# Decoder layer on one Trainium2 core: attention loop laid out anew, twelve units of maxima ahead, times-V product in front of the scores

## The reference, cut to what matters

```
x = layernorm(x + attn_block(x))          # gives x1
x = layernorm(x + xattn(x, ctx))          # gives x2
x = layernorm(x + experts(x))
# xattn, 16 heads of 8 features:
q = rope(layernorm_per_head(x @ q_w.T + q_b)) * scale
k = layernorm_per_head(ctx @ k_w.T + k_b);  v = ctx @ v_w.T + v_b
o = softmax(q @ k.T) @ v
return o @ out_w.T + out_b
```

## Time and profile before

| what | value |
|---|---|
| median of 3 runs | 373.38 us (371.13 to 375.3) |
| the profiled execution's own time | 370.08 us |
| its span, first to last instruction | 368.0 us |
| mean granted TensorE clock | 0.853 |
| PE busy, share of span | 276.7 us, 75% |
| DVE busy | 186.6 us, 51% |
| ACT busy | 154.7 us, 42% |
| POOL busy | 95.6 us, 26% |

### The profile page before, as it was taken

How to read it: one execution, slowest core, us unless ns; L and a number is a source line. 1 busy time by engine, 2 the same in 40 slices (tenths; PEclk the granted TensorE clock), 3 DMA queues, 4 the chain that set the end, 5 groups by cost and what they waited for, 6 DMA issues and landing times.

```text
span 368.0 us, 7297 instructions
## 1 busy us (share of the span) xinstructions
PE 276.7 (75%) x2437; PEld 210.3 (57%) x2437; DVE 186.6 (51%) x660; ACT 154.7 (42%) x365; POOL 95.6 (26%) x126
## 2 busy tenths in 40 slices
PE   1798967589799268899876988741058999999880
PEld 0588755447558135344443545431055999999880
DVE  4541556611153475654797596557100656566560
ACT  2233244455783425654672465410107443434330
POOL 2000036204232222220341403105100343535341
PEclk9999998599899666955995699865559999999996
DMA  7700025305993944335055000001864000000000
GB/s 221 234 2 1 0 62 144 52 0 133 233 285 97 215 109 116 49 89 89 2 152 80 32 3 18 16 2 37 198 177 112 7 14 21 16 15 15 5 14 14
DMA packets 30529, 28.34 MB, mean 77 GB/s; under 512 B 2829, under 2 KB 27024, under 8 KB 30498
## 3 DMA queue, kind: packets, MB, share of 16 engines
q1 hardware_dynamic: 28884, 25.24, 28.9%
q0 software_dynamic: 1328, 2.66, 2.2%
q10 hardware_dynamic: 288, 0.07, 0.1%
HBM read 17.85 MB, written 10.37 MB: 77 GB/s over the span
## 4 chain that ended last, share of the span: by engine, by line
PE 54%; DVE 12%; DMA 11%; ACT 9%; issue 8%; POOL 3%; SPq 1%; POOLq 0%; ACTq 0%; DVEq 0%
PE ps L796 7%; PE ps L787 7%; PE ps L669 4%; DMA out_dram<-ADD,tok_u 4%; PE ps L647 4%; PE ps L385 3%; DVE M L1135 3%; PE ps L556 3%; PE ps L685 2%; PE ps L416 2%; DMA WA<-in_attn_w_dram 2%; PE ps L457 2%; PE ps L393 2%; DMA QPK<-q_packed_scratch 2%; PE ps L707 2%
## 5 line engine op out<-in xcount | busy, mean ns | idle before, releaser
L1135 DVE TENSOR_REDUCE M<-ps 128x4 f32<-128x512 f32 x64 | 43.2, 687 | 30.2 <-PE ps L614 29.9
L962 ACT ACTIVATE CTX<-ps 128x512 f32<-128x512 f32 x64 | 38.1, 599 | 35.8 <-PE ps L647 27.2
L1003 ACT ACTIVATE KPK<-ps,EB 128x128 f32<-128x128 f32 x80 | 24.7, 359 | 41.7 <-PE ps L787 41.7
L796 PE MATMUL ps<-EW,KPK 128*128 128x128 f32 x320 | 40.1, 278 | 0.9 <-ACT KPK L1003 0.8
L1311 DVE TENSOR_SCALAR KPK<-ps,EB 128x128 f32<-128x128 f32 x80 | 22.5, 344 | 34.6 <-PE ps L787 34.4
L787 PE MATMUL ps<-QPK,EW 128*128 x320 | 39.1, 275 | 0.8 <-ACT QPK L988 0.8
L796 PEld LDWEIGHTS ps<-EW,KPK 128*128 128x128 f32 x320 | 38.1, 191 | 1.3 <-ACT KPK L1003 1.0
L787 PEld LDWEIGHTS ps<-QPK,EW 128*128 128x128 f32 x320 | 37.3, 192 | 1.0 <-issue 1.0
L647 PE MATMUL ps<-QPK,KPK 49*128 49x128 bf16 x256 | 28.9, 243 | 8.2 <-DVE M L1135 6.1
L614 PE MATMUL ps<-KPK,QPK 48*128 48x128 bf16 x256 | 27.9, 251 | 8.7 <-DMA QPK<-q_packed_scratch 5.6
L1406 POOL DMA_INDIRECT out_dram<-ADD,tok_u x21 | 21.1, 1004 | 46.3 <-DVE ADD L1304 43.6
(11 more groups left out here) (185 smaller groups left out, 531.5 us busy)
## 6 DMA issues: line engine op xcount, KB each, us to landing
k_packed_scratch<-PART SPq DMA_DIRECT2D x24, 128.0 KB, 2.4
KPK<-k_packed_scratch SPq DMA_DIRECT2D x8, 384.0 KB, 6.4
q_packed_scratch<-PART SPq DMA_DIRECT2D x24, 128.0 KB, 2.4
QPK<-q_packed_scratch SPq DMA_DIRECT2D x8, 384.0 KB, 5.8
KPK<-sorted_scratch SPq DMA_DIRECT2D x13, 198.0 KB, 4.1
EW<-in_eW_dram SPq DMA_DIRECT2D x1, 2048.0 KB, 11.9
sorted_scratch<-XW SPq DMA_DIRECT2D x8, 198.0 KB
X<-in_x_dram SPq DMA_DIRECT2D x4, 256.0 KB, 4.3
```

The lines of the kernel that those rows point to most:

```text
L796: last = mm(ps[:, 4, 0:P], HE[:, c, :], EW2[:, e, c % NF, :], start=(c == 0), stop=(c == 2 * NF - 1))
L962: A(EXPS[:, u % 4, :], ps[:, 2 + u % 2, :], ACT.Exp).then_inc(s_exp, 1)
L1003: last = A(HE[:, c, :], ps[:, k, (c % 2) * P:(c % 2 + 1) * P], ACT.Relu, bias=EB1[:, h, c:c + 1])
L1135: nc.vector.tensor_reduce(M[:, b % RING, c:c + 4], bank_rows(u % 2), AX.X, ALU.max).then_inc(s_max, 1)
```

## The change

Before the loop the maxima of `LEAD` = 12 units are done, and the whole query chains of groups 1, 2 and 3, in an order written out by hand; the two `keep_clock(3)` are gone there. Group 1's rotation goes into the last part of the GELU network's second product, with one more pair of activation table loads around it on ACT. In the loop `times_v(u - 2)` stands in front of `scores(u, u + LEAD)`. `max_T` and `negate_max` are for batch b+2 in unit r = 1 (before: batch b+1 in r = 0). `results_T(b - 2)` is in r = 0 (before: `results_T(b - 1)` in r = 3). `rows_T`, `project`, `ranks` and DVE's steps for the finished groups move one to three units later, and `whole_parts` of group 2 moves behind the loop. The load of the experts' second matrix (EW2) moves behind all the queries' DMAs in SP's list. On POOL the chains of groups 2 and 3 come before `x1_plus_bias(2)`, the load of the experts' bias and its arithmetic. Some PSUM banks change (`head_bank`, `var_bank`, `x1_bank`, `rot_bank`), with the waits that go with them.

```diff
-AHEAD = 2
+LEAD = 12
...
             for g in range(G):
                 write_parts(1, g)
                 read_packed(1, g)
-                if g == 0:
-                    sp.wait_ge(s_f2, G)
-                    sp.dma_start(EW2[:, :, :, :], ...).then_inc(ld_exp, 16)
+            sp.wait_ge(s_f2, G)
+            sp.dma_start(EW2[:, :, :, :], ...).then_inc(ld_exp, 16)
...
                         queries(1)
+                    if j == 2 and g == 3:
+                        rotate(1)
                 last.then_inc(s_f2, 1)
...
             pe.wait_ge(s_g1, NF * G)
-            for b in range(AHEAD):
-                for r in (0, 2):
-                    scores_for_max(4 * b + r)
-                    if (b, r) == (1, 0):
-                        queries(2)
-                if b == 1:
-                    x1_T(3)
-                keep_clock(3)
-                max_T(b)
-                if b == 0:
-                    rotate(1)
-                    x1_T(2)
+            x1_T(2)
+            queries(2)
+            scores_for_max(0)
+            scores_for_max(2)
+            x1_T(3)
+            variances(1, 2)
+            scores_for_max(4)
             queries(3)
+            max_T(0)
+            scores_for_max(6)
+            variances(1, 3)
+            rotate(2)
+            scores_for_max(8)
+            max_T(1)
+            scores_for_max(10)
+            rotate(3)
             for u in range(4 * B):
                 b, r = divmod(u, 4)
-                scores(u, u + 4 * AHEAD)
                 if u >= 2:
                     times_v(u - 2)
-                for g in range(2, G):
-                    if (b, r) == (q_batch(g), 1):
-                        pe.wait_ge(s_negm, b + AHEAD)
-                        variances(1, g)
-                    if (b, r) == (q_batch(g) + 1, 0):
-                        pe.wait_ge(s_lv[1], g + 1)
-                    if (b, r) == (q_batch(g) + 1, 1):
-                        pe.wait_ge(s_negm, b + AHEAD)
-                        rotate(g)
-                    if (b, r) == (q_batch(g) + 2, 0):
-                        pe.wait_ge(s_t2, g + 1)
-                if r == 1 and b > 2 * GB and b % GB == 1:
-                    pe.wait_ge(s_negm, b + AHEAD)
-                    ranks(b // GB - 2)
-                if r == 0 and b > 2 * GB and b % GB == 2:
-                    pe.wait_ge(s_ranked, b // GB - 1)
-                if r == 0 and 1 <= b and b + AHEAD - 1 < B:
-                    max_T(b + AHEAD - 1)
-                if r == 1 and b > GB and b % GB == 1:
-                    rows_T(b // GB - 1)
-                if r == 1 and b > GB and b % GB == 2:
-                    project(b // GB - 1)
-                if r == 3 and b >= 1:
-                    results_T(b - 1)
+                scores(u, u + LEAD)
+                if r == 0 and b >= 2:
+                    results_T(b - 2)
+                if r == 1 and b + 2 < B:
+                    if b > 2 * GB and b % GB == 2:
+                        pe.wait_ge(s_ranked, b // GB - 1)
+                    max_T(b + 2)
+                if r == 2 and b > GB and b % GB == 1:
+                    rows_T(b // GB - 1)
+                if r == 2 and b > GB and b % GB == 2:
+                    project(b // GB - 1)
+                if r == 3 and b > 2 * GB and b % GB == 1:
+                    pe.wait_ge(s_negm, min(b + 3, B))
+                    ranks(b // GB - 2)
             times_v(4 * B - 2)
             times_v(4 * B - 1)
+            results_T(B - 2)
             results_T(B - 1)
...
# ACT, in front of the last GELU of the second product
+                if g == G:
+                    nc.scalar.preload_act_table_set(LN_EXP)
+                    head_inv_std(1, 1)
+                    inv_std(2, 2, 1e-5)
...
# DVE
             first_sum(2)
+            head_norm(1, 1, QBC)
+            normalise_x1(2)
+            add_rotation(1)
             first_sum(3)
-            head_norm(1, 1, QBC)
...
-            for u in range(4 * AHEAD):
+            for u in range(LEAD):
                 maxima(u)
-                if u == 3:
-                    normalise_x1(2)
-                if u == 4:
-                    add_rotation(1)
+                if u == 1:
+                    normalise_x1(3)
                 if u == 5:
-                    normalise_x1(3)
+                    head_norm(1, 2, QBC)
+                if u == 7:
+                    add_rotation(2)
+                    head_norm(1, 3, QBC)
+                if u == 9:
+                    add_rotation(3)
```

More of the change, by code:

```diff
@@ L962, in _ @@
                 A(EXPS[:, u % 4, :], ps[:, 2 + u % 2, :], ACT.Exp).then_inc(s_exp, 1)
+                if u == 0:
+                    middle_part(1, 2)
                 if u == 1:
-                    square(1, 3, s_qc, QBC)
-                for g in range(2, G):
-                    if (b, r) == (q_batch(g), 1):
-                        head_inv_std(1, g)
-                    if (b, r) == (q_batch(g) + 1, 2):
-                        high_part(1, g)
-                    if (b, r) == (q_batch(g) + 2, 0):
-                        middle_part(1, g)
-                if r == 0 and 1 <= b and b + AHEAD - 1 < B:
-                    negate_max(b + AHEAD - 1)
+                    high_part(1, 3)
+                if u == 4:
+                    middle_part(1, 3)
+                if r == 1 and b + 2 < B:
+                    negate_max(b + 2)
                 if r == 2 and b >= 1:
                     copy_results(b - 1)
-                if r == 1 and b > GB and b % GB == 1:
+                if r == 3 and b > GB and b % GB == 1:
                     copy_oT(b // GB - 1)
-                if r == 1 and b > GB and b % GB == 3:
+                if r == 2 and b > GB and b % GB == 3:
                     inv_std_x2(b // GB - 1)
@@ L1221, in _ @@
             for u in range(4 * B):
                 b, r = divmod(u, 4)
-                if u + 4 * AHEAD < 4 * B:
-                    maxima(u + 4 * AHEAD)
-                for g in range(2, G):
-                    if (b, r) == (q_batch(g), 3):
-                        head_norm(1, g, QBC)
-                    if (b, r) == (q_batch(g) + 1, 1):
-                        add_rotation(g)
-                if r == 0 and b >= 2:
+                if u + LEAD < 4 * B:
+                    maxima(u + LEAD)
@@ L1231, in _ @@
+                if r == 1 and b >= 2:
                     attention_rows(b - 2)
[L1232 removed]
+                if r == 3 and b > GB and b % GB == 2:
                     add_x1(b // GB - 1)
[L1234 removed]
+                if r == 0 and b > GB and b % GB == 3:
                     mean_var(lambda b: blk(N, b), 3, b // GB - 1, s_y2)
[L1236 removed]
+                if r == 3 and b > GB and b % GB == 3:
@@ L1237, in _ @@
                     normalise_x2(b // GB - 1)
-                if r == 3 and b > GB and b % GB == 3:
-                    whole_parts(b // GB - 1)
-                if r == 1 and b >= 2 * GB and b % GB == 0:
+                if r == 0 and b >= 2 * GB and b % GB == 0:
+                    whole_parts(b // GB - 2)
+                if r == 2 and b >= 2 * GB and b % GB == 0:
                     experts(b // GB - 2)
-                if r == 3 and b >= 2 * GB and b % GB == 0:
+                if r == 0 and b > 2 * GB and b % GB == 1:
@@ L1243, in _ @@
                     count_experts(b // GB - 2)
-                if r == 2 and b > 2 * GB and b % GB == 1:
+                if r == 0 and b > 2 * GB and b % GB == 2:
                     place(b // GB - 2)
+            whole_parts(G - 2)
             attention_rows(B - 2)
@@ L1367, in _ @@
             query_affine(1)
+            low(1, 1, ADD, KP)
+            query_affine(2)
+            query_affine(3)
+            low(1, 2, ADD, KP)
+            low(1, 3, ADD, KP)
             x1_plus_bias(2)
-            low(1, 1, ADD, KP)
             x1_plus_bias(3)
@@ L1375, in _ @@
             nc.gpsimd.tensor_copy(X2[:, :, P:ROW], token_no[:, :, None].to_broadcast([P, B, ROW - P])).then_inc(s_x2id, 1)
-            for g in range(2, G):
-                query_affine(g)
-                low(1, g, ADD, KP)
             pool.wait_ge(s_qc, G)
```

45 lines of the change are left out of this document (24 added, 21 removed).

## The result

The changed kernel takes 375.38 us (median of 4 executions, 374.15 to 379.25) against 372.25 us of the kernel before (4 executions, 369.58 to 375.3): ratio 1.0216, 95% interval 1.015 to 1.0283. The forecast was 363.7 us, faster; it is slower, though not by much: the medians are 0.8% apart.

What follows compares the result with a forecast made beforehand. PE was taken as the bound at half clock, DVE at full clock. Case 1 summed +2.9 ahead of the loop, batches 28.8 - 35.1, -6.3 and -0.5, +0.5 behind: 373.4 - 9.7 = 363.7 us, range 356 to 378.

Steps and rivals of the forecast that it cites:

- case 1: Loop: clock low at the start, back about batch 3.5, then 1.00; -9.7 us, chance 0.35, the forecast.
- case 4: Loop: clock never back, or lost again; batches 6 to 12 take 48 us, 13 to 15 take 22; +12.3 us, chance 0.12.
- case 3: Loop: clock back only with ranks or projection in batch 9 or 10; +0.3 us, chance 0.18.
- the order put at nothing: Loop units: times-V before scores just covered at 1.00, 1.39 us against PE's 1.38; up to 6 us if semaphores take longer.
- `keep_clock(3)`: Ahead of the loop: removing the two saves PE some 3 us, but PE waits for DVE there anyway.
- DVE as the bound of batches 6 to 12 at 1.00: Batches 6 to 12: 5.35 us each, 37.5 in all, -6.3 us; sign: DVE over 90% busy.
- the stretch ahead of the loop: Before the loop: 17 to 22 us from a start at 126 to 127, so the loop starts 2.9 us later.
- A plain batch at 0.50: Loop: a batch with nothing extra costs PE 5.9 us at half clock; 4.2 at 1.00 with ACT's part.
- The wait for `copy_results`: Loop: `results_T` a batch behind its copy removes PE's 7.2 us of waits.
- the stall in `experts`: Batches 6 to 12: DVE's 1.5 us stall goes, since POOL's bias work comes earlier, at about 155 us.
- The mask row has 7 units to land: Loop: 7 units instead of 3, room for a DMA that now meets EW2's load; no wait for the row.

Runs made afterwards that it cites:

- before_no_keep_clock: The kernel before without its two `keep_clock(3)` ahead of the loop: 369.73 us, ratio 0.982.
- after_fill_loop: The changed kernel with sixteen unread 128x128 matmuls in PE's two waits ahead of the loop and every `results_T` transpose issued twice: 366.83 us, ratio 0.9927.
- scores_first_fill_front: The changed kernel with scores again ahead of times-V and sixteen unread 128x128 matmuls in PE's two waits ahead of the loop: 370.21 us.
- after_fill_front: The changed kernel with 8 unread 128x128 matmuls in each of PE's two waits for DVE ahead of the loop: 370.72 us, ratio 1.0015.
- after_lead8: The changed kernel with maxima 8 instead of 12 units ahead, so a mask row has 3 units to land: 384.16 us, ratio 1.0284.
- before_doubled: The kernel before with every transpose of `results_T` issued twice, nothing else: 363.15 us, ratio 0.9741.
- after_dense_back: The changed kernel with four unread 512-column products, one in each of batches 1 to 4: 370.9 us, ratio 1.0158.
- scores_first_filled: The changed kernel with scores again ahead of times-V, sixteen unread matmuls ahead of the loop and `results_T` transposes doubled: 357.25 us, ratio 0.9559.
- lead8_ew2_early: The changed kernel with maxima 8 instead of 12 units ahead and EW2's load back behind group 0's queries: 377.27 us.

## Why the prediction was wrong

**The step that failed first: the clock's course of case 1, in its second half.** It began as forecast: loop at 0.50, clock back at batch 4.6 (forecast 3.5). Then it said 1.00 for batches 6 to 12, and the clock fell at 193.3, was back at 207 behind the projection for 3.4 us, fell again at 210.4 and never came back in the loop. Batches 6 to 12 took 45.0 us, not 37.5, and 13 to 15 lost 5.1 instead of gaining 0.5. That is the second half of case 4 ("never back, or lost again") behind the first of case 1. Case 4's terms for it, 48 and 22 us, come nearer to the 45.0 and 20.0 than case 1's 37.5 and 15. It had a chance of 0.12, and case 1 0.35. I held the clock safe once a projection had raised it, and looked for a new cause of a fall only ahead of the loop. `results_T` a batch behind its copy was costed as the end of a wait. What was late next, the `add_x1` that frees its bank, stood PE still for 1.35 us right where the clock fell for good. That this wait did it was not tried, and two runs speak against it as the whole cause: in before_no_keep_clock the clock fell for good with no such wait, and in after_fill_loop it came back 7 us after a fall behind the same wait, 1.41 us long. The measured 375.38 us lies inside the stated range of 356 to 378 us, but by luck: the range reached up to case 3, a clock that comes back late and then stays, and that is not what happened.

**The second: the order put at nothing.** The prediction had 1.39 us round the loop against PE's 1.38, "just covered", with 0.1 a unit, 6 us, if semaphores take longer. Measured: 4.6 us in the changed kernel (375.38 against 370.82 us), ratio 1.0226 in the kernel before (medians 1.0044), 2.3 to 3% with doubled transposes. In a plain batch the prediction was nearly right: at half clock the order costs nothing (5.86 against 5.87 us), and at full clock some 0.24 us a batch, 0.06 a unit (3.86 to 3.89 us in scores_first_fill_front, 4.11 to 4.12 in batches 3 and 4 of after_fill_front). A balance of 1.39 against 1.38 holds only while nothing disturbs it. Whenever PE waits for an exponential (8 times in after_fill_front), ACT gets its next scores later by the length of the times-V; that nothing wins this back is my reading of the traces. By the fit, 1.3 to 1.7 us in the unfilled kernels are the order at an equal clock, and the rest would go through the clock; how it divides stays open, since the clock varies from one execution to the next.

**The third, small: `keep_clock(3)`.** The 3 us of PE that it takes were put at nothing, since PE would wait for DVE there anyway. Without it the kernel before is 0.9 to 1.8% faster.

**Half right: DVE as the bound of batches 6 to 12 at 1.00.** Batches 5 to 8 took 4.88 to 5.50 us against 5.0 to 5.35, but DVE was busy for 12.28 of the 15.71 us from 176.54 to 192.25, 78% and not the over 90% that the prediction names as its sign, and PE for 12.15. Neither engine was busy all the time.

**Right, in size as well:** the stretch ahead of the loop, 21.0 us from the first scores for maxima to the first exponential (before 17.1) where 17 to 22 was forecast, half clock at its end included; it began at 123.8 and not at 126 to 127, so the loop began 1.7 us later than before, not 2.9. A plain batch at 0.50: 166.07 - 160.21 = 5.86 us against 5.9. At 1.00: 3.9 to 4.3 against 4.2, seen in after_fill_front. The wait for `copy_results` gone, the stall in `experts` gone. "The mask row has 7 units to land" was right too (before it had 4, not 3), and after_lead8 shows what the lead is worth: with 3 units, 8.2 us of waits.

So most prices were right and the shares wrong: how much of the loop runs at which price. (One reading was a little off as well: of the kernel before's batches 6 to 12 nearly 14 us were at 0.50, not 12.) The clock in the loop had been read from one execution of a kernel whose executions span mean clocks of 0.798 to 0.893.

The Trainium skill (TensorE: Matmul & The Clock Gate, section on PSUM-queue depth-cycling) says of another kernel, one that cycles through PSUM banks, that TensorE's micro-idles between groups make the clock swing. The runs agree that it swings in this loop, but they also show it at 1.00 for 25 us on end of the same cycling (after_fill_front, 145 to 170 us), so the cycling alone does not decide.

## What to carry to other kernels

Where PE works at 1.2 GHz for part of its time, count the clock as a resource: ask of an edit that takes PE's dense work or leaves it waiting what the clock may lose, and look for it in the stages behind the edit too. Don't put a balance between two engines that comes out even at zero; let PE issue first what the next engine waits for (scores for ACT), and do its own backlog behind. Before anything else try a few unread products in PE's waits and between its groups, at places where nobody waits for PE, and time it: here that gave 2.0 to 2.6% for one line, and 3.5 to 4.4% together with the new layout in the old order. And take the spread of the clock from many executions before you forecast from one.

## What the runs showed of the hardware

- Work added to PE shortened the kernel: 64 needless transposes of 128x128 took before_doubled to 0.9741 of the kernel before, with the median of the mean granted clocks at 0.893 instead of the 0.844 of the kernel before in its group.
- At 0.50 PE can work without a gap, 32.31 of 32.60 us, and stay there; a full PE doesn't by itself bring the clock back. With one 512-column product of 2.08 us put in, it came back at 158.0 instead of 169.3 us (after_dense_back, one execution of each).
- The clock can be lost for the rest of the loop without a long wait of PE: in before_no_keep_clock it fell at 216.5 us, after waits of at most 0.81 us, and stayed at 0.50 with PE busy for 21.30 of 21.30 us.
- Executions of one program differ widely, and with their mean clock: the kernel before took 356.57 us at 0.893 and 378.37 us at 0.815, and the fit gives 2.0 us for 0.01.
- A 4 KB write by DMA that other runs hide kept PE waiting for 2.4 to 3.8 us while a 2 MB load was under way (after_fill_front, scores_first_filled, after_lead8), and for 3.2 and 3.4 us in after_lead8 and lead8_ew2_early while none was, beside the query parts' writes.
